# Four graph layers on one core: copies, negations, matmul runs and one layer's order moved between engines

## The chip, the cores and the metric

The kernel runs on one core of a Trainium2 chip. The metric is the device time of one execution in microseconds (us), the median of three runs. The engines are called by the names of the profile: PE (TensorE), with its weight loads as PEld, DVE (VectorE), ACT (ScalarE), POOL (GpSimd) and SP, which only issues transfers.

## The reference

The input is x of 8 batches x 1024 rows x 256 columns and, for each batch, a 1024 x 1024 matrix adj. Four layers follow one another, each as x = x + layer(relu(layernorm(x))):

```python
# layer 0: q, k, v from h; one weight per row
agg = adj @ (k * mask);  w = scale * mask * sum(q * agg);  out = softmax(w over rows) * v
# layer 1: 8 heads of width 32
scores = (q @ k.T) * scale * (adj + adj);  out = (softmax(scores) @ v) @ Wo.T + bo
# layer 2: H = (adj != 0)
out = Dn * (H @ (Be * (H.T @ (h @ W1.T)))) + b1, layernorm, relu, and the same with W2, b2
# layer 3: attention masked by adj, one head
```

## The kernel before

The batches are a loop of seven and a last one written out behind it. All five engines have an instruction list of their own and meet through semaphores; a `Signal` counts them over the batches. PSUM is one tensor `ps` of eight banks. P is 128, a tile t is 128 rows, NT is 8, DT is 2 (columns in pieces of 128) and NH is 2 (halves of 512 rows).

**Batch start (layer 0).** PE transposes the normalised rows h of the first half into banks 4 and 5 (`transpose_h`, L1015), then adj in 16 steps of four transposes (L1031), two steps to a tile row, one bank of 0 to 3 each. ACT copies the even steps out (L877), DVE the odd ones (L611). Ahead of step 4 PE waits for DVE's copies of the transposed rows (`hT_copies`, L594) and transposes the second half into banks 6 and 7. DVE's list begins with mask16 (L604) and the first `hT_copies`. Behind the adj steps stand the eight products with W0 (copied to G on ACT, L880), the eight adj products, reduced against G on DVE (L617), and a softmax over all rows: DVE multiplies by mask16 (L621), takes the maximum (L623), spreads it (L625), PE transposes it (L1054), DVE reduces, ACT takes the exponentials (L882). Queries and keys of layer 1 follow; SP stacks them by 30 transfers (L426).

**The units of layer 1.** A unit u is one row tile with one head; there are 64, and `STEPS` is 74 steps, in which every engine does its part of several units by the lags `INVERT`, `SPREAD`, `COPY`, `WEIGH`, `NORMALISE`, `PROJECT`, `ADD`. For a unit: PE makes two score products of 512 columns (`scores`, L1104), two units ahead; DVE multiplies by adj into Z (three buffers) with the row maximum in nm (L726) and negates it (L731); ACT takes the exponentials in place with their sums (L912); PE transposes Z in eight pieces into two of three banks (`transposes`, L1124); ACT copies the first half to PT (L904), DVE the second (L683), except that in each fourth unit ACT copies both (`BOTH`). Four units are a group g. Its sums are inverted on DVE (L687), spread on POOL (L496), brought to the rows by PE (`spread_inverses`, L1132) and copied to Rs by ACT ahead of that step's exponentials (L909). The weighted values of a group (`weighted_values`, L1146) are 128-row by 32-column matmuls, 4 for each of the eight kt, in three runs at the steps 4g+6, 4g+7 and 4g+8 of 3, 3 and 2 kt (`PARTS`), that is 12, 12 and 8 matmuls; each fp32 matmul stands as two in the trace. DVE normalises (L695), PE projects every second group (L983, Wo and ctxn). POOL writes the incidence H of a tile over adj in one instruction of 1024 columns (L505).

**Layer 3.** DVE adds the last result of layer 2 to x (L811) and takes statistics (L560, L565) tile by tile; POOL computes rstd by a power in two halves (`norm_scale`, L482 and L484), behind a wait for all eight sums of PE and a memset (L520); DVE forms nmr (`shift`, L572); ACT copies the product M3 out of `bank(0)` (L955) and then normalises eight tiles (L869). PE makes M3, two matmuls that keep it busy (`keep_warm`, L1007), waits for the copy, transposes, and goes on when DVE has copied the transposed rows (L594).

Of the kernel before, what the change touches and what calls it, by code (L numbers as in the profile page):

```python
# [7 lines left out]
ALU = mybir.AluOpType  # L8
# [23 lines left out]
def build_program(nc, x_in, adj_in, mask_in, wqkT0, wv0, w1attn, bq1, bk1, bv1, bo1,  # L32
# [13 lines left out]
    BOTH = 4  # L46
# [7 lines left out]
    with ctx:  # L54
# [25 lines left out]
        mhalf = sb("mhalf", [P, NT])  # L80
        mask = sb("mask", [P, NT])
# [130 lines left out]
        chain = signal("chain", 9)  # L212
# [86 lines left out]
        PARTS = (3, 3, 2)  # L299
# [168 lines left out]
        def _(pool):  # L468
# [6 lines left out]
            pool.wait_ge(consts_ready.sem, 4)  # L475
# [10 lines left out]
            def batch(b, last):  # L486
# [3 lines left out]
                for g in range(NT * GROUPS):  # L490

                    pool.wait_ge(*invs(b, g + 1))
# [5 lines left out]
                    if g % GROUPS == GROUPS - 1:  # L498

                        t = g // GROUPS  # L500
                        pool.wait_ge(*zs(b, HEADS * (t + 1)))
                        if t == NT - 2:
                            norm_scale(b, 2, 0)
                        stand(pool, waited_pool)
                        pool.tensor_scalar(H[:, t], adjN[:, t], 0.0, 0.0, ALU.is_equal, ALU.is_equal).then_inc(Hs.sem, 1)  # L505
# [26 lines left out]
        def _(dve):  # L532
# [19 lines left out]
            dve.wait_ge(consts_ready.sem, 4)  # L552
# [43 lines left out]
            def batch(b, last):  # L596
# [23 lines left out]
                dve.wait_ge(*chain(b, 1))  # L620
# [3 lines left out]
                dve.wait_ge(*chain(b, 3))  # L624
                dve.tensor_copy(E3[:, 1, 0:P], s1[:, 0:1].broadcast_to([P, P])).then_inc(wm_bc.sem, 1)  # L625
# [3 lines left out]
                dve.reciprocal(s1[:, 3:4], ps[:, 5, 0:1]).then_inc(chain.sem, 1)  # L629
                dve.wait_ge(*chain(b, 4))  # L630
# [703 lines left out]
```

## Time and profile before

| | us |
|---|---|
| median of three runs | 3336.92 (3333.25 to 3337.58) |
| the profiled execution | 3340.5 |
| its span, first to last instruction | 3337.7 |
| PE busy | 3172.0 (95%) |
| DVE busy | 2040.6 (61%) |
| ACT busy | 1524.3 (46%) |
| POOL busy | 577.5 (17%) |

The batch from 862.8 to 1275.3 us of the span is the one that is read closely. Matmuls are pipelined, so the starts of PE's instructions say more than their durations.

### The profile page before, as it was taken

What the parts mean: (1) busy time and instruction counts of PE and PEld (TensorE: products, weight loads), DVE (VectorE), ACT (ScalarE), POOL (GpSimd) and SP (SyncE); (2) the same over time, 40 slices, a digit from 0 to 9 for tenths busy, and PEclk for the clock granted to TensorE, in tenths of its full rate; (3) what the DMA queues carried; (4) which work ended last, traced back from release to release, by engine and by line L of the source; (5) the groups of instructions that cost most, each with busy time, mean ns of one, the idle gap of its engine ahead of it and who ended that gap; (6) DMA issues with size and microseconds to landing.
All of it is one profiled execution on the core that took longest, in us unless ns stands there. A gap on an engine that the chain in (4) does not pass through costs nothing.

```text
span 3337.7 us, 64889 instructions
## 1 busy us (share of the span) xinstructions
PE 3172.0 (95%) x23656; PEld 2450.6 (73%) x23656; DVE 2040.6 (61%) x4913; ACT 1524.3 (46%) x2881; POOL 577.5 (17%) x400
## 2 busy tenths in 40 slices
PE   6899998999989999899998999989999899998999
PEld 5677786777867778677776786767867678676786
DVE  2688426884368843687436874378743786437863
ACT  1584215842158431684316833168322683227722
POOL 0123001230012300123001230012300122001320
PEclk8999999999999999999999999999999999999999
DMA  3301203012030020300203002030020301112000
GB/s 109 77 2 33 73 14 77 2 33 73 14 77 2 33 73 14 77 2 33 73 14 77 2 33 73 14 77 2 33 73 18 73 2 43 62 39 52 24 10 13
DMA packets 75103, 135.44 MB, mean 41 GB/s; under 512 B 8592, under 2 KB 43792, under 8 KB 74768
## 3 DMA queue, kind: packets, MB, share of 16 engines
q1 hardware_dynamic: 74768, 131.01, 13.9%
q8 instruction: 206, 3.38, 0.4%
q14 instruction: 129, 1.06, 0.1%
HBM read 72.26 MB, written 8.39 MB: 24 GB/s over the span
## 4 chain that ended last, share of the span: by engine, by line
PE 80%; SPq 7%; issue 4%; DVE 4%; ACT 3%; DMA 1%; POOL 0%; ACTq 0%; DVEq 0%; POOLq 0%
PE ps L983 35%; PE ps L1184 14%; PE ps L1124 14%; SPq L426 7%; PE ps L1146 6%; PE ps L1104 5%; PE ps L1031 2%; PE ps L1132 1%; ACT h L869 1%; DVE hT L594 1%; PE ps L1015 1%; ACT Z L912 1%; DMA qS<-qlo 1%; DVE stats L560 0%; ACT h2T L938 0%
## 5 line engine op out<-in xcount | busy, mean ns | idle before, releaser
L726 DVE CUSTOM_DVE_ANT_0 Z<-ps,adjN 128x1024 f32<-128x1024 f32 x512 | 621.2, 1213 | 64.9 <-PE ps L1104 47.3
L1124 PE MATMUL ps<-ident,Z 128*128 128x128 f32 x4096 | 569.7, 283 | 74.3 <-ACT Z L912 43.6
L912 ACT ACTIVATE Z<-Z,nm 128x1024 f32<-128x1024 f32 x512 | 587.4, 1147 | 29.5 <-DVE nm L731 27.6
L1124 PEld LDWEIGHTS ps<-ident,Z 128*128 128x128 f32 x4096 | 458.7, 143 | 188.6 <-issue 98.5
L904 ACT ACTIVATE PT<-ps 128x512 f32<-128x512 f32 x640 | 364.1, 590 | 84.5 <-PE ps L1124 47.7
L1104 PE MATMUL ps<-kS,qS 128*128 128x512 f32 x1024 | 374.0, 450 | 6.8 <-ACT qS L894 6.8
L1146 PE MATMUL ps<-PT,v 128*32 128x128 f32 x8192 | 303.9, 279 | 0.0
L1146 PEld LDWEIGHTS ps<-PT,v 128*32 128x32 f32 x8192 | 205.6, 110 | 131.9 <-issue 130.7
L683 DVE COPY PT<-ps 128x512 f32<-128x512 f32 x384 | 264.2, 688 | 41.6 <-DMA qS<-qlo 21.7
L496 POOL TENSOR_SCALAR rs<-sm 128x128 f32<-128x128 f32 x128 | 68.2, 533 | 1080.2 <-DVE sm L687 1080.2
L505 POOL TENSOR_SCALAR H<-adjN 128x1024 fp32r<-128x1024 f32 x64 | 233.4, 3646 | 0.0
L983 PE MATMUL ps<-v,P 128*128 128x257 f32 x1024 | 223.6, 380 | 0.0
L983 PE MATMUL ps<-mh,adjT 128*128 128x256 f32 x1024 | 222.3, 380 | 0.0
L983 PE MATMUL ps<-hT,t3T 128*128 128x512 f32 x512 | 221.0, 593 | 0.0
L983 PEld LDWEIGHTS ps<-v,P 128*128 128x128 f32 x1024 | 194.2, 190 | 31.5 <-issue 3.8
L983 PEld LDWEIGHTS ps<-mh,adjT 128*128 128x128 f32 x1024 | 195.1, 191 | 25.9
L482 POOL TENSOR_SCALAR ve<-mv 128x4 f32<-128x4 f32 x80 | 15.7, 197 | 1116.9 <-DVE mv L565 1115.4
L983 PEld LDWEIGHTS ps<-hT,t3T 128*128 128x128 f32 x512 | 97.5, 190 | 118.8 <-issue 118.4
L617 DVE CUSTOM_DVE_ANT_0 E<-ps,G 128x256 f32<-128x256 f32 x64 | 27.2, 425 | 246.5 <-PE ps L983 246.5
L1104 PEld LDWEIGHTS ps<-kS,qS 128*128 128x128 f32 x1024 | 165.8, 198 | 14.6 <-issue 10.0
L983 PE MATMUL ps<-W,hT 128*128 128x256 f32 x768 | 174.3, 381 | 0.0
L966 ACT ACTIVATE E<-ps,cj 128x512 f32<-128x512 f32 x128 | 87.9, 687 | 187.4 <-PE ps L983 187.4
(165 smaller groups left out, 5395.6 us busy)
## 6 DMA issues: line engine op xcount, KB each, us to landing
adjN<-adj_in SPq DMA_DIRECT2D x8, 4096.0 KB, 15.9
kS<-khi SPq DMA_DIRECT2D x48, 256.0 KB, 3.8
kS<-klo SPq DMA_DIRECT2D x48, 256.0 KB, 5.0
qS<-qhi SPq DMA_DIRECT2D x96, 128.0 KB, 3.0
qS<-qlo SPq DMA_DIRECT2D x96, 128.0 KB, 3.1
xn<-x_in SPq DMA_DIRECT2D x8, 1024.0 KB, 6.1
out<-x SPq DMA_DIRECT2D x8, 1024.0 KB, 4.9
W1h<-w1T SPq DMA_DIRECT2D x9, 512.0 KB, 5.7
```

The source lines that it names most:

```text
L426: sp.dma_start(to.bitcast(F32), src[HD * j:HD * j + HD, :, cols].bitcast(F32)).then_inc(done.sem, 16)
L505: pool.tensor_scalar(H[:, t], adjN[:, t], 0.0, 0.0, ALU.is_equal, ALU.is_equal).then_inc(Hs.sem, 1)
L683: dve.tensor_copy(PT[:, u % PTS, NT // 2:NT], heads_of(ps[:, bank])).then_inc(PT_dve.sem, 1)
L726: dve.tensor_tensor_reduce(Z[:, u % ZS], ps[:, 2 * (u % 2):2 * (u % 2) + 2].rearrange("p a n -> p (a n)"), adjN[:, u // HEADS], SCORE_SCAL ...
L904: act.activation(PT[:, u % PTS, first:first + NT // 2], heads_of(ps[:, bank]), ACT.Copy).then_inc(PT_act.sem, 1)
L912: act.activation(Z[:, u % ZS], Z[:, u % ZS], ACT.Exp, bias=nm[:, u:u + 1], accum_out=sm[:, u:u + 1]).then_inc(exps.sem, 1)
L966: act.activation(E3[:, n % 2], ps[:, n % 4], ACT.Exp, bias=cj[:, n % NT:n % NT + 1]).then_inc(e3s.sem, 1)
L983: mm = pe.matmul(dst, lhsT, rhs, start=(i == 0), stop=(i == len(pairs) - 1))
L1104: mm = pe.matmul(ps[:, 2 * (u % 2) + s], qS[:, hd, rows(t)], kS[:, hd, half(s)], start=True, stop=True)
L1124: mm = pe.transpose(ps[:, turn_bank((u, s)), rows(a)], Z[:, u % ZS, rows(NT // 2 * s + a)], ident[:])
L1146: mm = pe.matmul(ps[HD * j:HD * j + HD, 7, 0:P], v[:, kt, HD * hd:HD * hd + HD], PT[:, (HPG * g + j) % PTS, kt], start=(kt == 0), stop=(kt ...
L1184: mm = pe.matmul(dst(n, i), lhs(n, j, i), rhs(n, j, i), start=(j == 0 and i == 0), stop=(j == NT - 1 and i == 0))
```

## The change

Two items touch layer 0, two the units and one layer 3.

- `BOTH` is 6 in place of 4, `PARTS` is (4, 4) in place of (3, 3, 2).
- The negation moves from DVE to POOL, as a product with a column of minus ones; POOL's list for the units is written step by step, with H in eight pieces, one per unit of the next tile.
- ACT copies the transposed rows at the batch start; PE waits for `mhs` (all of DVE's mask products, which stand at the end of DVE's previous batch) ahead of the second transposes.
- mask16 is the scale of the copies to G; the maximum of seven tiles is taken ahead of the eighth.
- Layer 3: POOL's norm_scale ahead of its wait and memset, `shift` of the first half ahead of the last addition, ACT's first four tiles ahead of the M3 copy, M3 in `bank(2)`, transposes in place of `keep_warm`.

```diff
-    BOTH = 4
+    BOTH = 6
-        PARTS = (3, 3, 2)
+        PARTS = (NT // 2, NT // 2)
...
 # gpsimd
+            pool.memset(minus[:], -1.0).then_inc(consts_ready.sem, 1)
...
-                for g in range(NT * GROUPS):
...
-                        pool.tensor_scalar(H[:, t], adjN[:, t], 0.0, 0.0, ALU.is_equal, ALU.is_equal).then_inc(Hs.sem, 1)
+                def negate_max(u):
+                    pool.wait_ge(*zs(b, u + 1))
+                    pool.tensor_tensor(nm[:, u:u + 1], nm[:, u:u + 1], minus[:], ALU.mult).then_inc(nms.sem, 1)
+                def spread_sums(g):
...
+                def incidence(t, of):
+                    done = pool.tensor_scalar(H[:, t, of], adjN[:, t, of], 0.0, 0.0, ALU.is_equal, ALU.is_equal)
+                    if of.stop == N:
+                        done.then_inc(Hs.sem, 1)
+                for u in range(STEPS):
+                    if u < UNITS:
+                        negate_max(u)
+                    if (g := group_due(u, INVERT)) is not None:
+                        spread_sums(g)
+                    if u == UNITS - 1:
+                        norm_scale(b, 2, 0)
+                    if HEADS <= u < UNITS:
+                        incidence(u // HEADS - 1, rows(u % HEADS))
+                    if u == UNITS:
+                        incidence(NT - 1, slice(0, N))
...
+                norm_scale(b, 4)
                 pool.wait_ge(*a4_ps(b, NT))
                 pool.memset(v3[:, :, D:HW], 1.0).then_inc(ones_col.sem, 1)
-                norm_scale(b, 4)
...
 # vector
-                hT_copies(b, 0, 0)
                 for n in range(1, NT * NH, 2):
-                    if n == 5:
-                        hT_copies(b, 0, 1)
...
+                    if t == NT - 1:
+                        dve.wait_ge(*wrs(b, NT - 1))
+                        dve.reduce_max(s1[:, 0:1], sw[:, 0, 0:NT - 1], AX.X).then_inc(chain.sem, 1)
...
-                dve.tensor_tensor(sw[:, 1], sw[:, 0], mask16[:], ALU.mult).then_inc(chain.sem, 1)
-                dve.reduce_max(s1[:, 0:1], sw[:, 1], AX.X).then_inc(chain.sem, 1)
-                dve.tensor_copy(E3[:, 1, 0:P], s1[:, 0:1].broadcast_to([P, P])).then_inc(wm_bc.sem, 1)
+                dve.tensor_scalar(E3[:, 1, 0:P], sw[:, 0, NT - 1:NT].broadcast_to([P, P]), s1[:, 0:1], None,
+                                  ALU.max).then_inc(wm_bc.sem, 1)
...
-                    if u < UNITS:
-                        dve.wait_ge(*zs(b, u + 1))
-                        dve.tensor_scalar(nm[:, u:u + 1], nm[:, u:u + 1], -1.0, None, ALU.mult).then_inc(nms.sem, 1)
...
+                    if t == TPH + 3:
+                        shift(b, 4, 0)
                     if t < NT:
                         dve.wait_ge(*a4_ps(b, t + 1))
...
-                    if t == TPH + 3:
-                        shift(b, 4, 0)
...
 # scalar
+                hT_copies(0)
                 for n in range(0, NT * NH, 2):
+                    if n == 4:
+                        hT_copies(1)
...
-                    act.activation(G[:, t], ps[:, 4 + t % 2, 0:D], ACT.Copy).then_inc(gs.sem, 1)
+                    act.activation(G[:, t], ps[:, 4 + t % 2, 0:D], ACT.Copy, scale=mask16[:, t:t + 1]).then_inc(gs.sem, 1)
...
+                normalise(b, 4, x, range(TPH))
                 act.wait_ge(*m3_ps(b, 1))
-                act.activation(M3[:].rearrange("p c d -> p (c d)"), ps[:, bank(0)], ACT.Copy).then_inc(m3s.sem, 1)
-                normalise(b, 4, 2, x)
+                act.activation(M3[:].rearrange("p c d -> p (c d)"), ps[:, bank(2)], ACT.Copy).then_inc(m3s.sem, 1)
+                normalise(b, 4, x, range(TPH, NT))
...
 # tensor
                     if n == 4:
-                        pe.wait_ge(*hTs(b, DT))
+                        pe.wait_ge(*mhs(b, NT))
                         transpose_h(b, 0, 1)
...
-                keep_warm(bank(1), 2)
+                transpose_h(b, 2, 0)
                 pe.wait_ge(*m3s(b, 1))
-                transpose_h(b, 2, 0)
```

## Rows read from the trace of the kernel before

**Rows 1.** The page: engines' busy time, and the chain that ended last.

```profile
PE 3172.0 (95%) x23656; PEld 2450.6 (73%) x23656; DVE 2040.6 (61%) x4913; ACT 1524.3 (46%) x2881; POOL 577.5 (17%) x400
PE 80%; SPq 7%; issue 4%; DVE 4%; ACT 3%; DMA 1%; POOL 0%; ACTq 0%; DVEq 0%; POOLq 0%
```

**Rows 2.** Busy by stretch: us, PE, PEld, DVE, ACT, POOL; clock, DMA share, GB/s.

```profile
1024.70:1042.60 17.90, 17.64 (x217) 13.61 (x217) 15.97 (x38) 14.82 (x28) 4.68 (x3) 1.00 0.01 2
```

**Rows 3.** PE's timeline in one group of units: start, us, instruction.

```profile
1033.62 0.39 PE L1132 MATMUL ps<-ident,rs 128*128 128x128 f32 x2
...
1035.58 1.09 PE L1124 MATMUL ps<-ident,Z 128*128 128x128 f32 x8 [0.25 <-ACT Z L912]
...
1037.07 0.86 PE L1146 MATMUL ps<-PT,v 128*32 128x128 f32 x24
1037.86 1.09 PE L1124 MATMUL ps<-ident,Z 128*128 128x128 f32 x8
1038.71 0.71 PE L1104 MATMUL ps<-kS,qS 128*128 128x512 f32 x2
1039.35 0.65 PE L1146 MATMUL ps<-PT,v 128*32 128x128 f32 x16
1039.92 1.09 PE L1124 MATMUL ps<-ident,Z 128*128 128x128 f32 x8
1040.77 0.71 PE L1104 MATMUL ps<-kS,qS 128*128 128x512 f32 x2
1041.32 1.03 PE L1124 MATMUL ps<-ident,Z 128*128 128x128 f32 x8
```

**Rows 4.** ACT's timeline among the units.

```profile
1029.99 1.08 ACT L904 ACTIVATE PT<-ps 128x512 f32<-128x512 f32 x2 [0.49 <-PE ps L1124]
...
1034.05 0.28 ACT L909 ACTIVATE Rs<-ps 128x128 f32<-128x128 f32 x1 [1.36 <-PE ps L1132]
```

**Rows 5.** Who waited for whom, whole span: us in total, times, longest.

```profile
ACT Z L912 <- DVE nm L731: 27.6, 36, 2.5
...
DVE mask L604 <- issue: 15.1, 6, 2.7
```

**Rows 6.** DVE's negation, and POOL's nearest small instructions, from the timeline.

```profile
1028.06 0.15 DVE L731 TENSOR_SCALAR nm<-nm 128x1 f32<-128x1 f32 x1
...
1199.57 0.19 POOL L482 TENSOR_SCALAR ve<-mv 128x4 f32<-128x4 f32 x1
1199.85 1.01 POOL L484 TENSOR_TENSOR rstd<-ve,mhalf 128x4 f32<-128x4 f32 x1
```

**Rows 7.** Timeline at the start of a batch, and the adj transposes of the last.

```profile
866.30 0.17 DVE L604 TENSOR_SCALAR mask<-mask 128x8 f32<-128x8 f32 x1 [2.38 <-issue]
...
867.84 1.48 PE L1015 MATMUL ps<-ident,h 128*128 128x128 f32 x8 [2.16 <-DVE hT L594]
...
875.69 7.07 PE L983 MATMUL ps<-W,hT 128*128 128x256 f32 x32
...
2927.68 5.40 PE L1031 MATMUL ps<-ident,adjN 128*128 128x128 f32 x48
```

**Rows 8.** Busy by stretch at the same batch start (columns as in Rows 2).

```profile
870.00:872.00 2.00, 2.00 (x12) 2.00 (x11) 0.79 (x2) 0.68 (x2) 0.00 (x0) 0.54 0.00 0
872.00:874.00 2.00, 2.00 (x21) 2.00 (x20) 1.38 (x2) 1.41 (x3) 0.00 (x0) 1.00 0.00 0
```

**Rows 9.** Timeline: DVE from the last reduction to the spread maximum.

```profile
910.99 0.17 DVE L621 TENSOR_TENSOR sw<-sw,mask 128x8 f32<-128x8 f32 x1
...
911.39 0.23 DVE L625 COPY E<-s 128x128 f32<-128x128 f32 x1
```

**Rows 10.** PE's timeline behind the last unit.

```profile
1102.22 0.46 PE L1132 MATMUL ps<-ident,rs 128*128 128x128 f32 x2 [0.51 <-DVE ctxn L695]
```

**Rows 11.** Timeline of layer 3's start.

```profile
1202.21 1.01 POOL L484 TENSOR_TENSOR rstd<-ve,mhalf 128x4 f32<-128x4 f32 x1
...
1205.27 1.99 PE L983 MATMUL ps<-hT,M 128*128 128x512 f32 x4 [0.94 <-DVE hT L594]
```

More of the change, by code:

```diff
@@ L80, in build_program @@
         mhalf = sb("mhalf", [P, NT])
+        minus = sb("minus", [P, 1])
         mask = sb("mask", [P, NT])
@@ L211, in build_program @@
         wrs = signal("wrs", NT)
-        chain = signal("chain", 9)
+        chain = signal("chain", 8)
         wm_bc = signal("wm_bc", 1)
@@ L629, in batch @@
                 dve.reciprocal(s1[:, 3:4], ps[:, 5, 0:1]).then_inc(chain.sem, 1)
+                dve.wait_ge(*chain(b, 3))
+                dve.tensor_scalar(sw[:, 3], sw[:, 2], s1[:, 3:4], None, ALU.mult).then_inc(chain.sem, 1)
                 dve.wait_ge(*chain(b, 4))
-                dve.tensor_scalar(sw[:, 3], sw[:, 2], s1[:, 3:4], None, ALU.mult).then_inc(chain.sem, 1)
-                dve.wait_ge(*chain(b, 5))
                 dve.wait_ge(*x_free(b, 1))
@@ L770, in batch @@
                 dve.tensor_scalar(dn[:, 2], dn[:, 0], TINY, None, ALU.max).then_inc(chain.sem, 1)
+                dve.wait_ge(*chain(b, 6))
+                dve.reciprocal(dn[:, 3], dn[:, 2]).then_inc(chain.sem, 1)
                 dve.wait_ge(*chain(b, 7))
-                dve.reciprocal(dn[:, 3], dn[:, 2]).then_inc(chain.sem, 1)
-                dve.wait_ge(*chain(b, 8))
                 dve.tensor_tensor(dn[:, 3], dn[:, 3], dn[:, 1], ALU.mult).then_inc(chain.sem, 1)
                 dve.wait_ge(*w2_in(b, 48))
-                dve.wait_ge(*chain(b, 9))
+                dve.wait_ge(*chain(b, 8))
                 dve.wait_ge(*xh(b, 2))
@@ L863, in _, with normalise @@
         def _(act):
-            def normalise(b, l, k, src):
-                for t in range(NT):
+            def normalise(b, l, src, tiles=range(NT)):
+                for t in tiles:
                     if t % TPH == 0:
@@ L872, in batch, with hT_copies @@
             def batch(b, last):
+                def hT_copies(s):
+                    for c in range(DT):
+                        act.wait_ge(*hT_ps(b, s * DT + c + 1))
+                        act.activation(hT[:, c, half(s)], ps[:, 4 + 2 * s + c], ACT.Copy).then_inc(hTs.sem, 1)
+                hT_copies(0)
                 for n in range(0, NT * NH, 2):
+                    if n == 4:
+                        hT_copies(1)
                     act.wait_ge(*aT_ps(b, n + 1))
@@ L879, in batch @@
                     act.wait_ge(*g_ps(b, t + 1))
-                    act.activation(G[:, t], ps[:, 4 + t % 2, 0:D], ACT.Copy).then_inc(gs.sem, 1)
+                    if t == 0:
+                        act.wait_ge(*chain(b, 1))
+                    act.activation(G[:, t], ps[:, 4 + t % 2, 0:D], ACT.Copy, scale=mask16[:, t:t + 1]).then_inc(gs.sem, 1)
                 act.wait_ge(*nwms(b, 1))
-                act.activation(sw[:, 2], sw[:, 1], ACT.Exp, bias=s1[:, 1:2], accum_out=s1[:, 2:3]).then_inc(es.sem, 1)
-                normalise(b, 1, 1, x)
+                act.activation(sw[:, 2], sw[:, 0], ACT.Exp, bias=s1[:, 1:2], accum_out=s1[:, 2:3]).then_inc(es.sem, 1)
+                normalise(b, 1, x)
                 for n in range(2 * GROUPS * NH):
@@ L989, in _ @@
             mm.then_inc(setup_pe.sem, 1)
-            pe.wait_ge(consts_ready.sem, 4)
+            pe.wait_ge(consts_ready.sem, 5)
             pe.wait_ge(beta_bc.sem, 2 * FT + DT)
@@ L1257, in batch @@
                 sum_up(*of_nodes(Vh, Vl), (v2s,), [v2s(b, t + 1) for t in range(NT)], a4_ps, tail=4)
-                pe.wait_ge(*x2f(b, 2))
+                pe.wait_ge(*x2f(b, 3))
                 pe.wait_ge(*w3_in(b, 48))
                 for c in range(DT):
-                    mm = product(ps[:, bank(0), D * c:D * (c + 1)], [(W3[:, 1, o, rows(c)], W3[:, 0, o]) for o in range(DT)])
+                    mm = product(ps[:, bank(2), D * c:D * (c + 1)], [(W3[:, 1, o, rows(c)], W3[:, 0, o]) for o in range(DT)])
                 mm.then_inc(m3_ps.sem, 1)
-                keep_warm(bank(1), 2)
+                transpose_h(b, 2, 0)
                 pe.wait_ge(*m3s(b, 1))
-                transpose_h(b, 2, 0)
                 pe.wait_ge(*x2f(b, NT))
```

17 lines of the change are left out of this document (4 added, 13 removed).

## The prediction

> **What bounds the kernel.** I read the page first: PE is busy 95% of the span, and 80% of the chain that ended last is PE [rows 1]. That alone doesn't say that less work on PE shortens anything, since starts and waits count as busy, so I read the stretches. Among the units, one period of eight takes 17.9 us; PE is busy 17.64 of them, DVE 15.97, ACT 14.82 and POOL 4.68 [rows 2]. PE is the bound there, with DVE 11% behind. PE's timeline of one group shows what a step costs [rows 3]: eight transposes move it on by 0.85 us (1037.86 to 1038.71), the scores by 0.55 when transposes follow (1040.77 to 1041.32) and by 0.64 when weighted values follow (1038.71 to 1039.35); 24 of the latter take 0.79 and 16 take 0.57. Eight more cost 0.22, so 16 should take 0.44: a run costs 0.13 on leaving and 0.09 on entering, whatever its length. In this group PE also waited 0.25 us for ACT's exponentials: the spread of the inverses began at 1033.62, ACT copied it at 1034.05 after an idle 1.36 us [rows 4], then took the exponentials, and the transposes began at 1035.58, 1.96 us after the spread.
>
> At a batch start DVE does nothing for 2.38 us before its first instruction (the releaser is "issue": nothing that the profile shows), and PE stands 2.16 us for DVE's copies of the transposed rows [rows 7]. Six batch starts have this gap [rows 5]. [...]
>
> **The change part by part.**
>
> *Weighted values in two runs.* The third run goes, its eight matmuls go to the other two. A fixed 0.22 us is saved per group, 0.44 per period. In the group with the wait, the first run now lasts 0.22 longer inside the 1.96 us from spread to transposes, and so fills the wait of 0.25: another 0.22. That is 0.66 per period. Sixty-four units less the ramps are seven periods: 4.6 us per batch, 37 us over eight. The bounds: nothing, if DVE or ACT takes over (first rival), and 0.85 per period (48 us) if the whole wait goes and the starts tighten. I take 37, since what is left to DVE and ACT still fits, as the next two items say.
>
> At the end of the units PE waits 0.51 us for DVE's normalisation of the group before the last, which stood behind the third run [rows 10]. With the sums done one step earlier this goes: 4 us over eight batches, between 0 and 8.
>
> *Negation on POOL.* DVE loses 0.15 us per unit [rows 6], 1.2 per period. The way from the maximum to the exponentials gets a hop to another engine. POOL's nearest small instruction takes 0.19 us, its nearest with two tensors 1.01, but that one is a power [rows 6]; a product of one column is nearer to the first. With some 0.2 us for POOL to see the semaphore, the exponentials are ready to start 0.25 us later than now, 1.1 later at the far bound. What hides it: only 36 of 512 exponentials waited for the negation at all, 27.6 us together [rows 5]; the others found ACT busy or waiting for the spread. I cost it at nothing. If that cover went, 0.25 us on all 512 units would be 128 us. Queued on POOL behind a negation are the spread of the sums and a piece of H, which is an eighth of what is now one instruction; POOL has 13 us idle of 17.9 [rows 2], and the negation of the next unit is due about 2 us later.
>
> *ACT doubles each sixth unit.* Two copies on ACT take 1.08 us [rows 4], so one is about 0.54. ACT loses two thirds of a copy per period, 0.36 us, and DVE gains one of some 0.7, 0.5 us. DVE's sum per period is then 15.97 - 1.2 + 0.5 = 15.3, ACT's 14.5, against PE's new 17.2. The double copies now fall into two different steps of a group in turn; behind one of them the next exponentials start half a microsecond late, once in twelve units. I take nothing for it, and up to 0.3 us per twelve units as a bound (13 us in all).
>
> *Batch start.* ACT, idle then, copies the rows; PE no longer waits for them, but for the mask products, which DVE finishes before its gap. PE goes on with the second transposes and adj step 4 at once. Step 5 needs DVE's first copy of adj: DVE starts at 866.30 [rows 7], multiplies the mask and copies, done near 867.1. Eleven steps at the pace of the last batch (twelve steps in 5.40, 0.44 each) [rows 7] then end at 872.0; the products began at 875.69. The gain is 3.6 us where the clock had fallen, and about the wait of 2.1 where it had not; an estimate of 3.1 over six starts gives 19 us, between 12 and 22. The first batch and the last have no gap: nothing there. [...]
>
> *Maximum of layer 0.* Two small DVE instructions ahead of the spread go, from 910.99 to 911.39 [rows 9], 0.40 us on the way to the softmax and from there to the 30 transfers of layer 1. Their replacement stands ahead of the last sum. The scale on ACT's copies costs nothing, since a copy of G waits for PE. 3 us over eight, between 0 and 4.
>
> *Layer 3.* POOL's second power ended at 1203.22 and PE's product began at 1205.27, after an idle 0.94 us [rows 11]. With the first half normalised ahead of the M3 copy, the transposes are done before DVE is free; DVE is free when the second power has ended, which I put 0.35 us earlier. Then come nmr and two copies (some 1.45 us together): 1204.3 instead of 1205.27, a gain of 0.95 us, 8 us over eight. Bounds: nothing, and a loss of 0.8 per batch if the clock falls (second rival). M3's other bank and the memset moved behind the powers cost nothing: both are wanted microseconds later.
>
> The sum is 37 + 4 + 19 + 3 + 8 = 71 us. The profiled execution took 3340.5 us, its span 3337.7; less 71 it is 3269.5. The median of the runs shown lies 3.6 us lower: **3266 us**.
>
> **Rivals.**
>
> *1. The units don't get shorter* (chance 0.2). DVE and ACT have 11% and 17% of slack in the mean, but their long steps no longer fall where PE's do: two PE steps of a group are now long (0.64 + 1.01 + 0.85 = 2.5 us), two short (0.55 + 0.85 = 1.4). If PE waits in the short ones for exponentials, the 37 us are lost. For it speaks that PE already waited for them in [rows 3]; against it the 13% that DVE has left. The time is 3266 + 37 = 3303.
>
> *2. The clock falls in layer 3* (0.12). [...] Four microseconds at about that level lose 1.7 to 2: instead of a gain of 0.95 a loss of 0.8 per batch, 14 us: 3280.
> [...]
>
> *3. Slower: the hop through POOL comes onto the path* (0.06). If POOL's product of two tensors costs what its power does, exponentials start 1.1 us later. In steps where ACT has some 0.45 us of slack, one unit in four, PE's transposes then wait 0.64: 128 units of 0.64 are 82 us against the 71 gained: 3347. It decides from 0.07 us of unhidden hop per unit on, without the gain among the units (34 us over 512), or 0.14 with it. Against it speak the 36 of 512 and the 0.19 us of POOL's other small instruction.
> [...]
>
> *4. Nothing measurable changes* (0.03): rival 1 with the gain at the batch start lost too, because ACT's four copies now delay its adj copies; for that PE would have to wait for ACT, whose copies start earlier than DVE's.
>
> **How the numbers follow.** My forecast has 0.59. A measurement of this kernel tells about 0.2% (7 us) from no change. The range reaches from the upper bounds of the gains (48 + 8 + 22 + 4 + 8 = 90, which is 3247, with 8 us for what overlaps I can't see) to rival 1 with the loss in layer 3 (3303 + 14): 3239 to 3317. Left outside are rivals 3 and 4 and some surprises on both sides. Faster: 0.59 + 0.2 + 0.12 = 0.91, within 0.2% 0.03, slower 0.06.
>
> **What would show it.** A period of eight units of 17.2 us instead of 17.9, with PE runs of 32 weighted values and no run of 16; the first transposes behind a spread without a wait. POOL instructions of about 0.2 us, 512 of them, and the waits of ACT's exponentials for POOL under 100 us in sum. At the batch start of [rows 7], the products with W0 5.8 us behind DVE's first instruction instead of 9.4, at full clock. In layer 3, the first product 0.9 us sooner at clock 1.00. I would be wrong if exponentials wait for POOL in most units, if DVE's additions for the batch start come before its gap no more, or if PE's stands among the units grow by what the runs save.

## The result: 1.5% faster where 2.1% was forecast, and the profile after

The changed kernel takes 3287.14 us (median of 4 runs, 3284.91 to 3288.5) against 3337.25 for the kernel before on the same chip (3333.25 to 3340.31). The ratio is 0.985, with a 95% interval of 0.9833 to 0.9867. The forecast was 3266 us, so the sign and the range held and 21 us of the gain did not come. Of the 71 us of the sum, the span shows 51.6 (3337.7 to 3286.1). All ratios in this document are of executions at the usual clock; one of the ten of b_both6 below took 4553 us at a mean granted clock of 0.654 and is left out of its ratio.

The page of the changed kernel, busy time by engine, the chain that ended last, and two groups of instructions, the exponentials and the negation (busy us, mean ns of one, idle us before it):

```profile
PE 3136.6 (95%) x23624; PEld 2455.7 (75%) x23624; DVE 1963.8 (60%) x4409; ACT 1519.3 (46%) x2865; POOL 741.1 (23%) x1305
PE 72%; DVE 9%; SPq 7%; issue 5%; ACT 4%; DMA 1%; POOL 1%; DVEq 0%; ACTq 0%; POOLq 0%
L932 ACT ACTIVATE Z<-Z,nm 128x1024 f32<-128x1024 f32 x512 | 587.4, 1147 | 24.8 <-POOL nm L495 24.6
...
L495 POOL TENSOR_TENSOR nm<-nm,minus 128x1 f32<-128x1 f32 x512 | 97.2, 190 | 727.2 <-DVE nm L739 726.6
```

The negation on POOL takes 190 ns, as priced, and the exponentials waited for it 24.6 us in all, where they had waited 27.6 us for DVE's [rows 5]. PE's share of the chain is lower than in [rows 1], 72% against 80%, and it says nothing of the gain: the chain goes through DVE more in layer 2, a stretch that took as long as before (744.1 and 743.7 us), and the fastest kernel below, a_ph8, shows 80% again.

To see where the time went I cut each of the eight batches at the starts of seven instructions that both kernels have, and added up each stretch over the batches. The sums are in us, each from one profiled execution:

| stretch, from ... to | before | after | difference | forecast |
|---|---|---|---|---|
| PE's first transpose of a batch to the products with W0 | 96.15 | 76.06 | -20.1 | -19 |
| first product with adjT to the first stacking transfer | 421.79 | 418.39 | -3.4 | -3 |
| that transfer to the copy to PT that waits for qS | 267.23 | 275.48 | **+8.2** | 0 |
| that copy to PE's first product of layer 2 | 1097.64 | 1054.40 | -43.2 | -41 |
| layer 3, M3's products to the first t3T product | 49.96 | 44.62 | -5.3 | -8 |
| that product to the next batch (seven) | 490.81 | 502.28 | **+11.5** | 0 |
| behind it in the last batch | 70.21 | 71.91 | **+1.7** | 0 |

Layer 2, the products with W0 and the head of the program differ by 0.9 us together. So the five rows with a forecast came out within 3 us each, and two things were missed: 13 us behind layer 3's start, and 8 us in the stacking of layer 1's queries and keys. (The stacking is 36 transfers a batch, not 30 as the text ahead of this section has it: 48 of each of khi and klo and 96 of each of qhi and qlo over eight batches. 30 is the number of rows in SP's timeline, which puts pairs together.)

**Batch start**, against [rows 7, 8]. The timeline of PE and DVE, then the busy time by stretch (us, PE, PEld, DVE, ACT, POOL; clock, DMA share, GB/s):

```profile
850.38 1.11 PE L1036 MATMUL ps<-ident,h 128*128 128x128 f32 x8
...
859.46 7.07 PE L1004 MATMUL ps<-W,hT 128*128 128x256 f32 x32
...
853.73 0.17 DVE L620 TENSOR_SCALAR mask<-mask 128x8 f32<-128x8 f32 x1 [2.36 <-issue]
```

```profile
850.00:852.00 2.00, 2.00 (x17) 1.62 (x16) 0.91 (x3) 0.90 (x2) 0.00 (x0) 1.00 0.04 12
...
854.00:856.00 2.00, 1.95 (x19) 1.71 (x17) 1.83 (x3) 1.56 (x4) 0.00 (x0) 1.00 0.70 232
```

DVE's gap of 2.36 us is still there; PE no longer stands behind it, the products begin 5.73 us after DVE's first instruction (forecast 5.8, before 9.4), and the clock reads 1.00 all through PE's nine microseconds of transposes (850.38 to 859.46). Before, it fell behind four of the six waits of this kind, and how often it falls differs between executions: the kernels below that keep the old batch start sum to 88 to 96 us, those with the new one to 75 to 78. So the gain lies between 11 and 21 us, and the table's 20.1 is near the upper end.

**The units**, against [rows 2, 3, 4]. Two periods of eight units, then a group on PE from its first run on, with ACT's share in it:

```profile
990.48:1007.67 17.19, 17.03 (x219) 13.76 (x217) 15.01 (x31) 14.19 (x27) 7.31 (x18) 1.00 0.01 2
...
1024.86:1041.85 16.99, 16.96 (x219) 13.74 (x218) 15.23 (x31) 14.08 (x27) 7.41 (x18) 1.00 0.01 2
```

```profile
991.90 1.08 PE L1167 MATMUL ps<-PT,v 128*32 128x128 f32 x32
992.91 1.10 PE L1145 MATMUL ps<-ident,Z 128*128 128x128 f32 x8
...
994.41 1.08 PE L1167 MATMUL ps<-PT,v 128*32 128x128 f32 x32
995.42 1.09 PE L1145 MATMUL ps<-ident,Z 128*128 128x128 f32 x8
996.27 0.72 PE L1125 MATMUL ps<-kS,qS 128*128 128x512 f32 x2
996.82 1.03 PE L1145 MATMUL ps<-ident,Z 128*128 128x128 f32 x8
997.61 0.71 PE L1125 MATMUL ps<-kS,qS 128*128 128x512 f32 x2
998.45 1.09 PE L1145 MATMUL ps<-ident,Z 128*128 128x128 f32 x8
...
996.11 1.09 ACT L924 ACTIVATE PT<-ps 128x512 f32<-128x512 f32 x2 [0.78 <-PE ps L1145]
997.08 1.15 ACT L932 ACTIVATE Z<-Z,nm 128x1024 f32<-128x1024 f32 x1
```

A run of 32 weighted values takes 1.01 us (994.41 to 995.42), and the group has two. The transposes behind the spread come 1.01 behind the run's start, without the wait of [rows 3]. But the last scores are followed by transposes after 0.84 us instead of 0.55: ACT copied both halves from 996.11 on, its next exponentials began only at 997.08 and took 1.15 us, and PE's last transposes came at 998.45, behind their end. A period of 17.19 holds one such stall, one of 16.99 none of that size; two in three are of the longer kind.

**Maximum of layer 0**, against [rows 9]. DVE's timeline:

```profile
891.21 0.16 DVE L628 TENSOR_REDUCE s<-sw 128x1 f32<-128x7 f32 x1
...
894.54 0.08 DVE L633 DVE_READ_ACCUMULATOR2_ANT sw<- 128x1 f32 x1
894.66 0.29 DVE L637 TENSOR_SCALAR E<-sw,s 128x128 f32<-128x128 f32 x1
```

The spread follows the last sum directly; 0.43 us per batch.

**Layer 3**, against [rows 11]. DVE's copy of the transposed rows and PE's product behind it, then the stretches around it:

```profile
1182.84 1.29 DVE L610 COPY hT<-ps 128x512 f32<-128x512 f32 x2 [0.29 <-issue]
...
1184.18 3.23 PE L1004 MATMUL ps<-hT,M 128*128 128x512 f32 x4 [1.83 <-DVE hT L610]
```

```profile
1182.00:1184.00 2.00, 0.35 (x4) 0.11 (x2) 1.32 (x3) 1.43 (x4) 0.41 (x2) 1.00 0.10 39
1184.00:1186.00 2.00, 1.82 (x3) 0.91 (x4) 0.13 (x1) 0.66 (x2) 0.00 (x0) 0.70 0.03 8
1186.00:1188.00 2.00, 2.00 (x6) 1.02 (x5) 0.00 (x0) 0.55 (x1) 0.00 (x0) 0.50 0.00 0
```

The four t3T products that took 1.99 us [rows 11] take 3.23 at a granted clock of 0.70 and then 0.50. Ahead of the fall PE had stood for 1.83 us. (The wait's last releaser is the copy at 1182.84.) This is what the second rival said, and it happens in seven of the eight batches: in six of them behind waits of 1.83 to 1.86 us and in the last behind one of 1.45. The first batch's wait of 1.84 us had no fall behind it.

### The profile page after: what moved, and what is told of

It is laid out like the page before. It is cut to its first block, busy times and chain, and to the rows that moved or that the text cites. A ratio compares the mean times of both kernels' runs of the same rounds, so it can differ in the third digit from the quotient of the medians.

```text
span 3286.1 us, 65469 instructions
## 1 busy us (share of the span) xinstructions
PE 3136.6 (95%) x23624; PEld 2455.7 (75%) x23624; DVE 1963.8 (60%) x4409; ACT 1519.3 (46%) x2865; POOL 741.1 (23%) x1305
## 3 DMA queue, kind: packets, MB, share of 16 engines
q14 instruction: 123, 1.01, 0.1%
## 4 chain that ended last, share of the span: by engine, by line
PE 72%; DVE 9%; SPq 7%; issue 5%; ACT 4%; DMA 1%; POOL 1%; DVEq 0%; ACTq 0%; POOLq 0%
PE ps L1004 33%; PE ps L1145 13%; PE ps L1205 10%; PE ps L1167 8%; SPq L427 7%; PE ps L1125 5%; DVE junk L775 2%; PE ps L1053 2%; DVE stats L576 1%; ACT Z L932 1%; DVE dn L784 1%; PE ps L1153 1%; POOL rstd L486 1%; DVE h L791 1%; DMA qS<-qlo 1%
## 5 line engine op out<-in xcount | busy, mean ns | idle before, releaser
L1145 PEld LDWEIGHTS ps<-ident,Z 128*128 128x128 f32 x4096 | 469.9, 145 | 190.4 <-issue 77.1
L932 ACT ACTIVATE Z<-Z,nm 128x1024 f32<-128x1024 f32 x512 | 587.4, 1147 | 24.8 <-POOL nm L495 24.6
L924 ACT ACTIVATE PT<-ps 128x512 f32<-128x512 f32 x592 | 342.5, 593 | 107.2 <-PE ps L1145 56.9
L696 DVE COPY PT<-ps 128x512 f32<-128x512 f32 x432 | 297.3, 688 | 108.6 <-PE ps L1145 74.7
L507 POOL TENSOR_SCALAR H<-adjN 128x128 fp32r<-128x128 f32 (+1 forms) x456 | 318.1, 698 | 0.0
L1167 PEld LDWEIGHTS ps<-PT,v 128*32 128x32 f32 x8192 | 214.3, 111 | 96.4 <-issue 89.7
L1167 PE MATMUL ps<-PT,v 128*32 128x128 f32 x8192 | 280.9, 279 | 4.5 <-DVE PT L696 4.5
L495 POOL TENSOR_TENSOR nm<-nm,minus 128x1 f32<-128x1 f32 x512 | 97.2, 190 | 727.2 <-DVE nm L739 726.6
```

Of the source, the lines that this page charges most:

```text
L495: pool.tensor_tensor(nm[:, u:u + 1], nm[:, u:u + 1], minus[:], ALU.mult).then_inc(nms.sem, 1)
L507: done = pool.tensor_scalar(H[:, t, of], adjN[:, t, of], 0.0, 0.0, ALU.is_equal, ALU.is_equal)
L696: dve.tensor_copy(PT[:, u % PTS, NT // 2:NT], heads_of(ps[:, bank])).then_inc(PT_dve.sem, 1)
L924: act.activation(PT[:, u % PTS, first:first + NT // 2], heads_of(ps[:, bank]), ACT.Copy).then_inc(PT_act.sem, 1)
L932: act.activation(Z[:, u % ZS], Z[:, u % ZS], ACT.Exp, bias=nm[:, u:u + 1], accum_out=sm[:, u:u + 1]).then_inc(exps.sem, 1)
L1145: mm = pe.transpose(ps[:, turn_bank((u, s)), rows(a)], Z[:, u % ZS, rows(NT // 2 * s + a)], ident[:])
```

## The experiments

All twelve kernels ran beside the kernel before; a ratio is to the runs of that kernel taken beside them. Three questions: which part of the change brings the gain among the units and why they stall, whether the clock explains layer 3, and what lengthens the stacking. The sums over the eight batches (us, cut as above) that the text draws on; "inner" is the part of the units from the first projection to the last. What lies ahead of the first projection differs by up to 15 us between kernels (150.7 to 166.0), in part with the time at a granted clock of 0.50 there (20 us in b_runs, 52 in a_both4); so the inner part tells more of an edit of the units than the whole:

| kernel | ratio | batch start | stacking | units | inner | layer 3 | behind it (7) | period of eight units |
|---|---|---|---|---|---|---|---|---|
| before | 1 | 96.2 | 267.2 | 1097.6 | 929.2 | 50.0 | 490.8 | 17.90 |
| after | 0.985 | 76.1 | 275.5 | 1054.4 | 889.4 | 44.6 | 502.3 | 16.98 to 17.20 |
| b_runs | 0.9925 | 91.8 | 266.5 | 1068.1 | 908.7 | 50.0 | 491.0 | 17.54 |
| b_neg | 0.9974 | 88.3 | 274.0 | 1086.5 | 920.9 | 50.0 | 492.5 | 17.66 |
| b_both6 | 1.0033 | 94.4 | 266.8 | 1109.9 | 946.9 | 49.9 | 490.4 | 17.95 to 18.35 |
| b_start | 0.9951 | 76.7 | 267.7 | 1101.6 | 929.2 | 50.0 | 492.3 | 17.90 |
| a_warm | 0.9814 | 76.5 | 272.6 | 1052.4 | 889.5 | 44.8 | 490.8 | 16.99 to 17.20 |
| a_both4 | 0.9887 | 75.9 | 273.2 | 1081.0 | 908.8 | 42.1 | 491.3 | 17.54 |
| a_negdve | 0.9845 | 77.6 | 272.3 | 1061.6 | 897.1 | 42.0 | 497.2 | 17.14 to 17.45 |
| a_stand | 0.9849 | 76.0 | 273.3 | 1053.3 | 889.5 | 44.6 | 501.7 | as after |
| b_shift | 1.002 | 95.1 | 272.5 | 1098.0 | 930.9 | 50.0 | 490.6 | 17.93 |
| a_end | 0.9792 | 75.2 | 266.7 | 1054.5 | 889.0 | 44.7 | 490.8 | 16.99 to 17.20 |
| a_ph4 | 0.9761 | 76.5 | 267.0 | 1047.2 | 884.1 | 42.8 | 490.3 | 16.98 |
| a_ph8 | 0.9722 | 74.7 | 267.4 | 1033.0 | 875.8 | 42.8 | 494.5 | 16.84 |

### One part alone

**b_runs** is the kernel before with the weighted values in two runs.

```diff
-        PARTS = (3, 3, 2)
+        PARTS = (NT // 2, NT // 2)
```

> The kernel before with the weighted values in two runs of 4 kt, all else as before (DVE still negates, ACT doubles each fourth unit). My working gives the period of eight units 0.66 us less than 17.90 and 0.5 us at the end of the units: about 17.2 and 41 us in all, 3296. If the shorter period needed the load taken off DVE (rival 1), it stays above 17.5 and the kernel above 3310. The stack of transfers, 33.4 us from its first issue to the copy that waited for it, should stay as it is.

It took 3311.53 us (ratio 0.9925, 0.9904 to 0.9946). The period is 17.54 us, a gain of 0.36 instead of the 0.66 that the forecast gave to this edit. PE and ACT in a group:

```profile
1393.57 0.71 PE L1104 MATMUL ps<-kS,qS 128*128 128x512 f32 x2
1394.42 1.09 PE L1124 MATMUL ps<-ident,Z 128*128 128x128 f32 x8
...
1392.08 1.09 ACT L904 ACTIVATE PT<-ps 128x512 f32<-128x512 f32 x2 [0.78 <-PE ps L1124]
1393.05 1.15 ACT L912 ACTIVATE Z<-Z,nm 128x1024 f32<-128x1024 f32 x1
```

Here every group has the stall (0.85 us from scores to transposes instead of 0.55), since every fourth unit is copied by ACT alone, and that is always the same unit of a group. Two stalls of 0.30 us a period are more than the 0.30 us that are missing of the 0.66; without them the period would be 16.94 us, 0.96 less than before and below what I had put as the bound (0.85). The first rival had named such waits in the short steps. Before, ACT's exponentials began as long behind the start of the double copy (1038.74 to 1039.70, 0.96 us, against 0.97 here), but the third run, which is gone, stood ahead of the transposes and filled that time [rows 3]. From the first projection to the last this edit alone gains 20.5 us.

**b_neg** moves the negation to POOL, with H in eight pieces.

```diff
+        minus = sb("minus", [P, 1])
...
+                def negate_max(u):
+                    pool.wait_ge(*zs(b, u + 1))
+                    pool.tensor_tensor(nm[:, u:u + 1], nm[:, u:u + 1], minus[:], ALU.mult).then_inc(nms.sem, 1)
...
-                        dve.wait_ge(*zs(b, u + 1))
-                        dve.tensor_scalar(nm[:, u:u + 1], nm[:, u:u + 1], -1.0, None, ALU.mult).then_inc(nms.sem, 1)
```

> The kernel before with the negation on POOL and H in eight pieces, all else as before. If the hop is hidden, as I costed it, the period stays at 17.9 us and the kernel within 0.2% of 3337. If the hop is on the path, 0.25 us for a unit would show as up to 2 us on the period. In the changed kernel the time from the first stacking transfer to the copy that waited for the last grew from 33.4 to 34.4 us in every batch; the theory that POOL's longer list of instructions or its work does this expects 34.4 here, about 8 us more in all; the theory that another part does it expects 33.4.

It took 3328.11 us (0.9974, 0.9963 to 0.9985). The units gain 11 us; the period is 17.66. The exponentials waited 21.4 us for POOL in all. The third rival, a hop on the path, finds nothing here that speaks for it. (Of the 11 us, 8 are in the inner part.) And the stacking is 7 us longer, with nothing changed there that one would name: this run is the first sign that the +8 comes with this part.

**b_both6** only lets ACT copy both halves in every sixth unit.

```diff
-    BOTH = 4
+    BOTH = 6
```

> The kernel before with ACT doubling each sixth unit. DVE gets 0.46 us more per period of 17.9 and keeps 1.4 idle: my theory, no change of the period, and no change of the kernel beyond 0.2%. The rival is that the double copies at a moving place disturb PE: period over 18.1 us. If the moving of the unit whose two halves ACT copies is what makes the stack of transfers longer, 34.4 us show here.

Alone it loses: 3349.41 us (1.0033, 1.0023 to 1.0043), with a period of up to 18.35; the inner part is 17.7 us longer. PE and DVE in such a period:

```profile
1422.60 0.39 PE L1132 MATMUL ps<-ident,rs 128*128 128x128 f32 x2
1423.45 1.13 PE L983 MATMUL ps<-Wo,ctxn 128*128 128x256 f32 x4 [0.46 <-DVE PT L683]
...
1422.71 0.69 DVE L683 COPY PT<-ps 128x512 f32<-128x512 f32 x1
```

DVE, with its negations still in its list, gets to the copy 0.1 us after PE's spread, and what PE does next waits for it. That the negations are what makes DVE late is argued, not shown: no run has this edit with the negation on POOL and nothing else.

**b_start** only moves the batch start's copies to ACT.

```diff
-                hT_copies(b, 0, 0)
...
+                hT_copies(0)
                 for n in range(0, NT * NH, 2):
+                    if n == 4:
+                        hT_copies(1)
...
-                        pe.wait_ge(*hTs(b, DT))
+                        pe.wait_ge(*mhs(b, NT))
```

> The kernel before with ACT copying the transposed rows of the batch start and PE waiting for the mask products. From the first transposes to the products with W0: about 9.1 us in the six batches that had 11.3 to 13.2, 20 us in all, 3317. The rival, that ACT's four more copies delay its adj copies, expects above 10 us. If the earlier start is what makes the stack of transfers longer, 34.4 us show here.

It took 3322.59 us (0.9951, 0.9933 to 0.9969) and its batch starts sum to 76.7 us, as in the changed kernel: the whole term is this edit. By the ratio it is worth 16 us (10 to 22). The stacking stays at 267.7.

### Parts of the changed kernel undone

**a_warm** puts two products that keep PE busy behind the transposes of layer 3. They write to `bank(3)`, so PE first waits until DVE has read that bank (`x2f` 4 in place of 3).

```diff
-                pe.wait_ge(*x2f(b, 3))
+                pe.wait_ge(*x2f(b, 4))
...
+                keep_warm(bank(3), 2)
```

> The changed kernel with two keep_warm matmuls behind the first transposes of layer 3, into a bank that nobody reads any more, so that PE works in the 1.8 us in which it stood. If the stand is what lets the clock fall to 1.2 GHz (rival 2), the clock stays at 1.00 there, the stretch from the first product of layer 3 to the next batch goes back from 71.9 to 70.05 us, and the kernel gains 1.85 us for each of eight batches, 15 us: 3272. If the clock has nothing to do with it, the stretch stays at 71.9.

It took 3273.05 us (0.9814, 0.9798 to 0.983), by the ratios 12 us below the changed kernel, and the stretches behind layer 3's start are those of before (490.8). The first t3T product and the granted clock at the same place:

```profile
1183.41 1.98 PE L1004 MATMUL ps<-hT,M 128*128 128x512 f32 x4
```

```profile
1182.00:1184.00 2.00, 1.88 (x6) 0.58 (x5) 1.29 (x2) 1.88 (x4) 0.00 (x0) 1.00 0.01 4
1184.00:1186.00 2.00, 2.00 (x12) 1.23 (x11) 0.14 (x1) 0.57 (x1) 0.00 (x0) 1.00 0.00 0
```

The first t3T product comes no sooner than in the changed kernel (44.8 us for eight against 44.6), and the clock now falls at this place in no batch, so the 12 us are what the fall had cost.

**a_both4** is the changed kernel with every fourth unit doubled, as before the change.

```diff
-    BOTH = 6
+    BOTH = 4
```

> The changed kernel with ACT doubling each fourth unit again. Alone, the two runs took 0.37 us off the period of eight units, the negation on POOL 0.24, and the sixth unit added 0.25; the changed kernel has 0.77 off. If the parts add, the period here is 17.90 - 0.61 = 17.29 or less, 16.9 if the sixth unit also costs 0.25 beside the others. If the sixth unit helps once DVE is relieved of the negation, the period is longer than the 17.12 of the changed kernel: up to 17.4, 15 us more in all.

It took 3298.25 us (0.9887, 0.9871 to 0.9904): its units are 27 us longer, 19 of them in the inner part, and the period is 17.54 us, that of b_runs. So in the company of the other parts every sixth unit is worth 19 us, where alone it cost 18. The time is only 12 us longer than that of the changed kernel, as layer 3's clock fell in none of the eight batches here, although PE stood 1.48 us before the product in each. DVE and PE there, against the lines of the changed kernel above:

```profile
1188.88 0.16 DVE L588 SCALAR_TENSOR_TENSOR nmr<-mv,rstd 128x4 f32<-128x4 f32 x1 [1.52 <-POOL rstd L486]
1188.98 1.29 DVE L610 COPY hT<-ps 128x512 f32<-128x512 f32 x2
...
1190.32 1.98 PE L1004 MATMUL ps<-hT,M 128*128 128x512 f32 x4 [1.48 <-DVE hT L610]
```

DVE's copy follows nmr at once. In the changed kernel DVE stood 0.29 us ahead of it, in each of the seven batches of the loop, for nothing that the profile shows ("issue"). That is the difference between a wait of 1.83 us and one of 1.48, and between 44.6 and 42.1 us for layer 3.

**a_negdve** puts the negation back on DVE, in the changed kernel; POOL keeps its wait for each unit.

```diff
-                    pool.tensor_tensor(nm[:, u:u + 1], nm[:, u:u + 1], minus[:], ALU.mult).then_inc(nms.sem, 1)
+                    stand(pool, waited_pool)
...
+                        dve.wait_ge(*zs(b, u + 1))
+                        dve.tensor_scalar(nm[:, u:u + 1], nm[:, u:u + 1], -1.0, None, ALU.mult).then_inc(nms.sem, 1)
```

> The changed kernel with the negation back on DVE; POOL still waits for each maximum, but in an instruction that only counts a semaphore. If the relief of DVE is what lets the two runs pay, the period of eight units goes from 17.12 to 17.5 or more, 3310 or above. If the moved negation was worth only its own 0.24, it is near 17.36, some 3300. The stack of transfers was 33.4 us before and 34.4 in both kernels that negate on POOL: if POOL's arithmetic instruction that waits is what slows SP's issues, it goes back to 33.4 here; if it is POOL's longer list, it stays at 34.4.

It took 3285.3 us, of which the interval is wide (0.9845, 0.9814 to 0.9876; 3271.22 to 3292.73 us). The units are 7 us longer than in the changed kernel, yet the median shows none of it: the stretches of layer 3 and behind it are 8 us shorter, since the clock fell less often (in five batches) and PE's wait there was shorter (1.47 us, DVE having no idle time ahead of its copy). Two batches of this one execution, PE and clock in each:

```profile
376.38 3.53 PE L1006 MATMUL ps<-hT,M 128*128 128x512 f32 x4 [1.47 <-DVE hT L610]
...
1186.99 1.98 PE L1006 MATMUL ps<-hT,M 128*128 128x512 f32 x4 [1.47 <-DVE hT L610]
```

```profile
376.00:378.00 2.00, 1.62 (x3) 0.64 (x4) 0.32 (x1) 1.21 (x3) 0.00 (x0) 0.67 0.04 10
378.00:380.00 2.00, 2.00 (x5) 0.86 (x4) 0.00 (x0) 0.05 (x1) 0.00 (x0) 0.50 0.00 0
...
1187.00:1189.00 2.00, 2.00 (x6) 1.00 (x7) 0.00 (x0) 0.82 (x2) 0.00 (x0) 1.00 0.04 8
```

The wait is 1.47 us in both, and the clock fell behind one of them and not behind the other.

**a_stand** lets POOL's queue do the waiting ahead of the negation by a semaphore increment, in place of the product itself.

```diff
+                    stand(pool, waited_pool)
                     pool.tensor_tensor(nm[:, u:u + 1], nm[:, u:u + 1], minus[:], ALU.mult).then_inc(nms.sem, 1)
```

> The changed kernel with one instruction more ahead of each negation on POOL: it takes the wait for the maximum and only counts a semaphore, so that the product itself waits for nothing. SP's issues of the stack ran at 0.69 us each instead of 0.64 while POOL's product waited. Theory: the product standing at POOL with an open wait slows them, so the stack goes back from 34.4 to 33.4 us and the kernel gains up to 8 us, less what the extra instruction adds to the hop (below 0.1 us). Rival: the wait has nothing to do with it, 34.4 as before.

Nothing moved: 3285.03 us (0.9849, 0.9832 to 0.9865), stacking 273.3. With a_negdve, whose POOL negates nothing and whose stacking is 272.3, the idea falls that the negations on POOL slow SP's issue. What is left in common is the one new tile of SBUF, `minus`: every kernel that has it behind mhalf stacks in 272 to 276 us, every kernel without it in 266 to 268.

### The place of a tile in SBUF

`minus` has one element a partition and is declared right behind mhalf, ahead of the four tiles that the transfers read (khi, klo, qhi, qlo) and of the two that they write (kS, qS). How far it moves them no trace shows; its place in that order is what the next two kernels change.

**b_shift** is the kernel before with that tile, which nothing uses. **a_end** is a_warm with `minus` as the last tile, so that nothing else moves.

```diff
         mhalf = sb("mhalf", [P, NT])
+        minus = sb("minus", [P, 1])
```

```diff
-        minus = sb("minus", [P, 1])
...
         (v,), (W1h, W2g), (xn,) = r1, r2, r3
+        minus = sb("minus", [P, 1])
```

> [...] Theory (the transfers of qhi, khi, qlo and klo from SBUF to SBUF cost more where their rows start 32 bytes off their old places): the stretch from the first of these issues to the last PT copy that waits for qS takes 34.4 us in each batch instead of 33.4, and the time is 8 us longer, about 3345. Rival (the stretch is longer because of what GpSimd and ScalarE do in the changed kernel): it stays at 33.4 us and the time stays that of before.

> The changed kernel with the two products that keep the clock up ahead of layer 3's transposes (as a_warm), and with minus as the last tile of SBUF, so that every other tile lies where it lay before the change. Theory (place in SBUF): the stacking stretch falls from 34.4 to 33.4 us in each batch and the time from 3273 to 3264.5 us. Rival (negations on GpSimd slow the issue of the transfers): 34.4 us and 3273 us.

b_shift took 3346.52 us, a ratio of 1.002 (1.001 to 1.0031), that is 7 us longer, and its stacking 272.5 us against 267.2. a_end took 3269.66 us (0.9792, 0.9776 to 0.9809) and stacks in 266.7 us. SP's timeline of the same transfers in the second batch, start, us, instruction; first before, then b_shift, then a_end:

```profile
521.75 1.32 SPq L426 DMA_DIRECT2D kS<-khi  x2
...
532.91 1.33 SPq L426 DMA_DIRECT2D qS<-qhi  x1
```

```profile
522.53 1.32 SPq L427 DMA_DIRECT2D kS<-khi  x2
...
534.20 1.39 SPq L427 DMA_DIRECT2D qS<-qhi  x1
```

```profile
512.07 1.32 SPq L427 DMA_DIRECT2D kS<-khi  x2
...
523.25 1.32 SPq L427 DMA_DIRECT2D qS<-qhi  x1
```

The thirteenth issue comes 11.16, 11.67 and 11.18 us after the first. In the mean over the batches the 24th issue is at 21.97 us before, 22.82 in b_shift and 21.97 in a_end; the twelve behind it lose nothing more. So 5 to 6 of the 8 us are shown to be the place of the tiles, and neither POOL nor ACT. The other 2 to 3 stay open: in its one profiled execution each, the kernels with `minus` behind mhalf stack in 272.3 to 275.5 us, and the changed kernel is the longest of them. Why the place counts no run shows, nor whether it is that of the tiles read or of those written, since `minus` stood ahead of both.

### Which unit ACT doubles

In the changed kernel, b_runs and a_both4 the stall of 0.3 us stands where ACT's double copy comes ahead of the exponentials for PE's second short step. The last two kernels move it by two units, so that it stands elsewhere in the group; they are built on a_end.

```diff
-    BOTH = 6
+    BOTH = 4
...
-            return u % BOTH == BOTH - 1
+            return u % BOTH == BOTH - 3
```

a_ph8 has 8 in the place of 4. The remainder of a doubled unit by four, its place in the group, is then 1 in both.

> As a_end, but ScalarE copies both halves of the transposed rows in every fourth unit, in those with a remainder of 1 instead of 3. Theory (what counts is which unit of eight pays the second copy: with a remainder of 3 ScalarE comes late to the exponential that the next short steps of TensorE wait for): the period of eight units is 17.1 us or less, against 17.54 with a remainder of 3, and the time is 3265 us or up to 8 us below. Rival (every fourth is too many copies for ScalarE wherever they stand): the period stays at 17.5 us and the time is about 3290 us.

> As a_ph4, with the second copy in every eighth unit (remainder 5), so that VectorE copies a half in seven of eight. Theory (place counts): a period of 16.9 to 17.1 us and about 3260 us. Rival (VectorE needs the relief of every sixth unit, as the gain of the changed kernel over the one with every fourth suggests it needs some balance): the period rises to 17.3 us or more, and the time is 3275 us or more.

a_ph4 took 3259.76 us (0.9761, 0.9745 to 0.9777) and a_ph8 3246.24 us (0.9722, 0.9705 to 0.9738). Every fourth unit with remainder 3 makes a period of 17.54 us, with remainder 1 one of 16.98: the same number of copies, 0.56 us apart. It is the place that costs. (The other edits of a_end leave the period of the changed kernel as it was.) a_ph8's period, and the last step of a group ahead of it:

```profile
997.72:1014.55 16.83, 16.80 (x219) 13.81 (x217) 15.29 (x31) 14.19 (x27) 7.40 (x19) 1.00 0.01 3
```

```profile
996.08 0.71 PE L1125 MATMUL ps<-kS,qS 128*128 128x512 f32 x2
996.62 1.03 PE L1145 MATMUL ps<-ident,Z 128*128 128x128 f32 x8
```

The last short step of the group has 0.54 us from scores to transposes, and PE stands 0.03 us of the whole period. DVE's 15.29 us, with a copy in seven of eight units, still leave it 1.5 us: the rival by which DVE needed the relief fell. a_ph8 beats both kernels, 1.3% below the changed one. Its stretches from layer 3 to the next batch are 4 us longer in sum than a_ph4's, as PE stood 1.4 us at three of its batch starts, for nothing that the profile shows (a stand like this came once in b_start and once in b_neg, too):

```profile
442.05 1.11 PE L1036 MATMUL ps<-ident,h 128*128 128x128 f32 x8 [1.41 <-issue]
```

## Why the prediction was right in sign and 21 us too low

**Weighted values in two runs** (forecast 37 us, and 41 with the end of the units; the inner part gained 39.8 by all edits together). The size came out, but not by the step as put. "What is left to DVE and ACT still fits" was read off sums of busy time; alone, the edit gave 0.36 us per period in place of 0.66, 20.5 us in all (b_runs), as ACT's double copy now falls in front of a short step of PE. The period reached 17.1 only because with every sixth unit the double copy meets such a step once in twelve units in place of once in four, an edit that I had costed at nothing: in this company it is worth 19 us. That the two errors nearly cancelled is luck. The bound of 13 us of loss that I gave it had the right mechanism (the next exponentials start half a microsecond late) and the wrong sign: what counts is how many of the short steps the double copy meets, and that fell.

**End of the units** (4 us). The last half period of a batch, up to the last projection, is 0.53 us shorter (8.96 to 8.43 in the batch read closely), 4 us in sum and part of the 39.8; b_runs has it too (8.38). The wait that the forecast removed was replaced by others, so the size is right and the step is not what was put. From the last projection to layer 2 nothing changed. The units' other 3.4 us lie ahead of the first projection, where kernels differ by up to 15 us, and are credited to no edit. PE's timeline at the end, for [rows 10]:

```profile
1082.31 1.96 PE L1167 MATMUL ps<-PT,v 128*32 128x128 f32 x64 [0.56 <-DVE PT L696]
1084.68 1.13 PE L1004 MATMUL ps<-Wo,ctxn 128*128 128x256 f32 x4 [0.41 <-DVE ctxn L708]
```

**Negation on POOL** (nothing). Right in the hop: 190 ns, and waits of 24.6 us in place of 27.6. The third rival's 1.01 us for the product did not come. In the inner part it is worth 8 us in two companies (a_negdve, b_neg) and nothing beside two runs with every fourth unit doubled (a_both4 908.8, b_runs 908.7), where the stalls set the period. It is not what makes every sixth unit pay: with the negation on DVE that edit still gains 12 us beside the two runs (908.7 in b_runs, 897.1 in a_negdve) and loses 18 beside the three (b_both6); b_runs and a_negdve differ in other parts too, but none of these lies among the units except POOL's H in eight pieces. The tile of the negation cost 5 to 6 us elsewhere.

**Batch start** (19 us) and **maximum** (3 us): right in place and mechanism, and in size as far as it can be told: 3.4 us for the maximum, and for the batch start 20.1 by the two executions compared and 16 by b_start's ratio.

**Layer 3** (8 us): the step that failed. The earlier start was there, 5.3 us instead of 8; the 8 come where DVE does not stand 0.29 us ahead of its copy (50.0 to 42.1 us in a_both4). But the gain of 0.95 us per batch was costed as if the clock stayed, and it did not: it fell in seven batches and gave back 13 us. I had the fall as a rival with its place and put 0.12 on it, though the waits of 2.2 to 2.6 us at the batch start were the nearest rows and the clock fell behind four of the six; a stand of 1.5 to 1.8 us deserved far more than 0.12. a_warm shows that the loss is the clock's, for with two products in the gap it is gone, and the other stretches stay within 3 us. The four microseconds at a lower clock that rival 2 counts with no run shows: in the batch read closely the clock reads 0.89, 0.50, 0.50, 0.50 and 0.90 in the five microseconds from 1184, 1.7 us lost, and the seven falls cost 13.2 us together, 1.9 each. A frequency, as a_warm's expectation has it, no run shows either; the profile gives the clock as a share, here 0.50. Rival 2's time, 3280 us, misses the result by 7 us, about what the stacking lost.

**Stacking** (not in the sum): the term that was missing. I priced a new tile of four bytes at nothing without a sentence on it. b_shift and a_end show 5 to 6 of the 8 us, the one by adding the tile ahead of those of the transfers (5.3 us in the stacking, 7 in the time), the other by putting it behind them (5.9 and 7). The 32 bytes of b_shift's expectation no run shows: what the kernels differ in is the place of the tile in the order, and with it the stacking, 272.5 us against 267.2.

The sum by measured terms: 43.2 + 20.1 + 3.4 + 5.3 + 0.9 - 8.2 - 13.2 = 51.5 us, and the spans differ by 51.6.

Open stays what the 0.29 us are for which DVE stands in layer 3 of the changed kernel, a_warm, a_stand and a_end and not in a_both4, a_negdve, a_ph4 and a_ph8; why the clock falls behind one wait and not behind another as long; the last 2 to 3 us of the stacking; and what the stands of 1.4 us at three batch starts of a_ph8 are. Of the 10 us between a_end and a_ph4, 2 are that stand of DVE and not the place of the copy.

## What to carry to other kernels

Where two engines take turns at a job, ask not only how often the second one takes it but in which step of the bounding engine's pattern: the same number of copies, two units further on, was worth 0.56 us of 17.5. Before an instruction that fills a wait of PE is taken out, look in the trace for a stand (PE doing nothing) of its new length with the clock behind it, and keep a filler unless the clock stayed up there: behind stands of 1.83 to 1.86 us it fell in six of seven batches here. And a new tile, however small, belongs behind all others, or its place is priced: with it ahead of the tiles of the transfers the stacking took 272.5 us in place of 267.2 (b_shift), with it last 266.7 (a_end).

## What the runs showed of the hardware that was not expected

- An unused tile of one element a partition, ahead of the tiles that they read and write, lengthens 36 transfers from SBUF to SBUF by 0.7 us of 33.4 (b_shift); the 24th issue comes 22.82 us behind the first in place of 21.97.
- The granted clock fell to 0.50 behind a wait of PE of only 1.47 us and stayed at 1.00 behind an equally long one, in one execution of one kernel (a_negdve: five falls in eight batches); behind 1.48 us it fell in none of eight (a_both4).
- The timing of a unit's copies decides more than an engine's share: b_both6 takes copies from ACT and is slower (1.0033), and a_ph8, with the fewest double copies of all, is the fastest (0.9722).
